# Decoder layer with routed experts: last block routed as two units, maxima loaded by ScalarE, w2 made the stationary operand, last expert by halves

## Chip, cores and metric
One core of a Trainium2 chip runs one program that does the whole layer. The metric is the device time of one execution in microseconds (us). Before the change the median of three runs is 755.97 us (755.29 to 756.68). Lower is better.

## What is computed
The reference is one decoder layer over 8 sequences of 256 tokens (2048 tokens, width 256). Three parts follow each other, each on the layer-normed sum of what came before:

```python
x = x + mixer(layernorm(x))            # projections, depthwise conv, cumprod/cumsum scan, gates
x = x + attention(layernorm(x), ctx, ctx)   # 16 heads of 16, causal, softmax over keys, output projection
xf = layernorm(x)                      # router and experts; the result is combined + xf
probs = softmax(xf @ router_w.T);  k_probs, k_idx = top_k(probs, 2)
rank  = running count of earlier pairs sent to the same expert;  keep = rank < 641
buf[expert, rank] = xf[token]          # 8 experts, 641 slots (648 in the kernel)
out_buf = silu(buf @ w1) @ w2          # w1 256x1024, w2 1024x256 for each expert
combined[token] = sum over its 2 experts of k_prob * out_buf[expert, rank]
```

The change touches the end of the attention stage, the routing and the experts. The mixer is as before.

## The kernel before
The engines have instruction streams of their own, written out by hand, and wait for each other by semaphores (`wait_ge`). Two functions follow each other: `mixer_and_projections` and `attention_route_experts`; all of the change lies in the second and in two small helpers.

**Attention** is a software pipeline over 48 steps `t`, three for each of 16 groups `g` (a sequence and half of its heads; `b` is a sequence, g = 2b or 2b + 1). In a step TensorE (PE) writes the masks, multiplies keys by queries into the bank `a_turned` (`turned`, L1538), computes the scores of the step six ahead (`scores`, L261), and multiplies probabilities by values (`weigh`, L1556). ScalarE (ACT) takes the exponential of `a_turned` (`exps`, L1420). There is one such bank, so the steps run in a ring: exponential, masks, `turned`, exponential. VectorE (DVE) takes the maxima of the scores six steps ahead (L275); every third step it turns them (L288), SyncE (SP) stores them to DRAM (`store_maxima`, L215), issues four large loads of queries and keys (`lay`, L208) and then loads the maxima as two extra query rows (`load_maxima`, L223), for which the first `turned` of that group waits.

At the end of a group DVE transposes the output bank (L1699), GpSimd (POOL) divides by the sums (`divide`, L1339), DVE turns back (L1707), and after two groups PE does the output projection of the sequence (`project`, L1573). The residual, the statistics, the power on POOL (L1328), the normed rows on ACT (L1425), their transposes on PE (`x3_turn`, L1583), the logits (L1593), the choice of two experts on DVE (`choose`, L1732 to L1746), the ranks on PE (`ranks`, L1603 and L1606), the slots (`place`) and the gates are done for blocks of four tiles of 128 tokens, `NBLK` = 4 blocks of two sequences. All of these share one PSUM bank (`a_shared`). A table of step offsets (`PROJECT`, `STATS`, ... `SEND`) says in which step an engine does each. Eight indirect DMAs for each block (`scatter`, L1349) then put the rows into the buffer `disp` in DRAM, and `base` (POOL, L1333) adds the residual that SP stores to `out`.

**Experts.** SP waits for all scatters, then fetches expert 0's rows (`fetch`). PE transposes them (`turn`, L1615), and for each expert goes through 8 pieces `f` of the hidden width: `hidden` (12 matmuls of 324 columns, L101), then `result` (L1649) of the piece before. All products are split in a high and a low part, three matmuls for one. `result` holds the activations as stationary operand, 108 slots at a time, and moves 256 columns of w2: 6 slot tiles x 3 = 18 matmuls a piece. ACT and DVE make silu and its high and low parts (L1457, L1802, L1463, L1808), POOL the odd low half (`low`, L1367) and the low part of the next expert's w1 (L1356). At an expert's end ACT and DVE scale the six tiles by the gate (L1472, L1814), and POOL adds them to `out` by six indirect DMAs (`give`, L1378), the first of which waits until those of the expert before have landed.

## Time and profile before
| | |
|---|---|
| median of three runs | 755.97 us |
| profiled execution, its own time | 752.37 us |
| its span (first to last instruction) | 750.7 us |
| PE, DVE, ACT, POOL busy | 83%, 65%, 46%, 44% |
| mean granted TensorE clock | 0.909 of full speed |
| mean DMA rate | 109 GB/s |
| mixer and projections | to about 270 us |
| attention and routing | about 270 to 470 us |
| experts on PE | about 470 to 734 us |
| last indirect DMAs | 737 to 751 us |

Busy time is the time in which an engine has an instruction in work. PE's matmuls overlap, so that the duration of one (283 ns for L1649) is longer than the distance to the next. A clock of 1.00 is 2.4 GHz, 0.50 is 1.2 GHz; the two are told apart by windows. "Idle before" at an instruction is the time that its engine had nothing to do, with what ended it. Times inside the trace are counted from the start of the span.

### The profile page before, as it was taken

Reading aid. Unit: us, or ns where it says so; the run is one execution under the profiler, and the core shown is the slowest. Engines: PE = TensorE matmul, PEld = TensorE weight load, DVE = VectorE, ACT = ScalarE, POOL = GpSimd, SP = SyncE. Lnnn points to the kernel's source line nnn. Section 1 sums busy time; section 2 is a strip of 40 time slices with the busy share of each in tenths; the row PEclk is TensorE's granted clock in tenths of the full one; section 3 lists DMA queues with packets and bytes.
Section 4 is the critical chain, followed back from the end, with each engine's and each line's share of the span. In section 5 each row is a group of like instructions: output and inputs, shape, how many; then the busy total and the mean of one; then the engine's idle time right before and its main releaser. Section 6 shows DMA issues by size and latency. Waiting matters only on the chain.

```text
span 750.7 us, 12394 instructions
## 1 busy us (share of the span) xinstructions
PE 623.4 (83%) x4408; PEld 524.0 (70%) x4408; DVE 490.3 (65%) x1017; ACT 343.3 (46%) x666; POOL 333.1 (44%) x321
## 2 busy tenths in 40 slices
PE   3586998988986788888889640999999999999991
PEld 2465887877774644555555430899999999999991
DVE  5686687796797545776756430477877777777630
ACT  4565563751633023353524310456555555665540
POOL 1234424233240051122352764245766868677665
PEclk9798999999999579998987855799999999999996
DMA  8301404855338746663661612405263452621123
GB/s 272 99 7 48 115 29 125 270 161 140 86 73 214 168 102 141 153 149 101 170 178 33 208 45 81 146 1 156 29 167 90 102 164 28 167 26 19 19 30 42
DMA packets 63197, 81.68 MB, mean 109 GB/s; under 512 B 10283, under 2 KB 47926, under 8 KB 63136
## 3 DMA queue, kind: packets, MB, share of 16 engines
q1 hardware_dynamic: 53920, 73.08, 34.7%
q0 software_dynamic: 9216, 7.81, 7.3%
q8 instruction: 35, 0.57, 0.3%
q14 instruction: 26, 0.21, 0.1%
HBM read 48.27 MB, written 34.36 MB: 110 GB/s over the span
## 4 chain that ended last, share of the span: by engine, by line
PE 42%; issue 5%; DMA 4%; DVE 4%; SPq 4%; POOL 3%; ACT 1%; POOLq 0%; DVEq 0%; ACTq 0%
PE w_bank L1649 16%; PE l_scores L101 10%; PE w_bank L101 5%; PE a_shared L1573 3%; DMA l_hi<-md 2%; POOL out L1378 2%; PE a_out L1556 2%; SPq L208 2%; PE a_turned L1538 2%; PE l_scores L1615 1%; PE a_shared L1593 1%; PE a_turned L1524 1%; DVE l_nm L275 1%; DMA w_rows<-disp 1%; PE l_scores L261 1%
## 5 line engine op out<-in xcount | busy, mean ns | idle before, releaser
L1649 PE MATMUL w_bank<-w_w2h,l_hi 128*108 128x256 f32 x384 | 108.5, 283 | 0.6 <-POOL l_lo L1367 0.5
L1649 PE MATMUL w_bank<-w_w2h,l_lo 128*108 128x256 f32 x384 | 107.7, 280 | 0.0
L1649 PE MATMUL w_bank<-w_w2l,l_hi 128*108 128x256 f32 x384 | 107.6, 280 | 0.0
L1367 POOL TENSOR_TENSOR l_lo<-w_v,l_hi 128x324 fp32r<-128x324 f32 x64 | 56.3, 879 | 91.7 <-ACT l_hi L1463 91.7
L1420 ACT ACTIVATE a_pr<-a_turned 128x1024 f32<-128x1024 f32 x48 | 49.2, 1024 | 88.4 <-PE a_turned L1538 88.4
L275 DVE TENSOR_REDUCE l_nm<-l_scores 128x4 f32<-128x1024 f32 (+1 forms) x48 | 58.5, 1218 | 37.9 <-PE l_scores L261 37.2
L1378 POOL DMA_INDIRECT out<-w_y,w_to x48 | 75.9, 1582 | 13.3 <-issue 9.9
L1802 DVE SCALAR_TENSOR_TENSOR w_v<-w_th,l_scores 128x324 f32<-128x324 f32 x86 | 42.3, 491 | 49.9 <-ACT w_th L1457 48.6
L1457 ACT ACTIVATE w_th<-l_scores 128x324 f32<-128x324 f32 x86 | 38.1, 442 | 68.6 <-PE l_scores L101 67.7
L1649 PEld LDWEIGHTS w_bank<-w_w2h,l_hi 128*108 128x108 f32 x384 | 66.0, 172 | 1.1 <-issue 1.1
L1463 ACT ACTIVATE l_hi<-w_v 128x324 fp32r<-128x324 f32 x128 | 60.4, 472 | 12.1 <-DVE w_v L1802 11.1
L1649 PEld LDWEIGHTS w_bank<-w_w2l,l_hi 128*108 128x108 f32 x384 | 65.9, 172 | 0.0
L1649 PEld LDWEIGHTS w_bank<-w_w2h,l_lo 128*108 128x108 f32 x384 | 65.9, 172 | 0.0
L1778 DVE TENSOR_TENSOR w_w2l<-w_s,w_w2h 128x256 fp32r<-128x256 f32 x56 | 62.2, 1110 | 1.9
L1356 POOL TENSOR_TENSOR w_w1l<-w_s,w_w1h 128x256 fp32r<-128x256 f32 x64 | 56.8, 888 | 0.0
L101 PE MATMUL l_scores<-l_hi,w_w1h 128*128 128x324 f32 x172 | 54.2, 315 | 1.1 <-ACT l_hi L1452 1.1
L101 PE MATMUL l_scores<-l_lo,w_w1h 128*128 128x324 f32 x172 | 54.4, 316 | 0.0
L101 PE MATMUL l_scores<-l_hi,w_w1l 128*128 128x324 f32 x172 | 54.4, 316 | 0.0
L1339 POOL TENSOR_TENSOR a_on<-a_po,a_rc 128x256 f32<-128x256 f32 x16 | 9.9, 619 | 95.1 <-DVE a_rc L1701 74.8
L101 PE MATMUL l_scores<-m_sh,l_hi 128*128 128x512 f32 x96 | 39.9, 416 | 10.3 <-ACT m_sh L565 6.9
L476 POOL TENSOR_TENSOR m_gl<-m_acc,m_gh 128x512 fp32r<-128x512 f32 x16 | 24.5, 1531 | 37.4 <-ACT m_gh L591 37.4
L467 POOL TENSOR_TENSOR m_rstd<-m_ve,c_mhalf 128x4 f32<-128x4 f32 (+1 forms) x7 | 8.3, 1188 | 70.9 <-DVE m_ve L118 70.9
(233 smaller groups left out, 1710.5 us busy)
## 6 DMA issues: line engine op xcount, KB each, us to landing
w_s<-in_L_ffn_w SPq DMA_DIRECT2D x14, 1024.0 KB, 5.0
l_lo<-kd SPq DMA_DIRECT2D x32, 200.0 KB
l_hi<-qd SPq DMA_DIRECT2D x32, 192.0 KB
disp<-c_blank SPq DMA_DIRECT2D x8, 658.1 KB
w_rows<-disp SPq DMA_DIRECT2D x8, 658.1 KB
kd<-l_qkh SPq DMA_DIRECT2D x16, 256.0 KB, 4.6
vd<-m_vf SPq DMA_DIRECT2D x4, 1024.0 KB, 6.8
qd<-l_qkh SPq DMA_DIRECT2D x16, 256.0 KB, 3.7
```

What stands on the lines that cost most here:

```text
L101: mm = pe.matmul(out, a, b, start=first and n == 0, stop=last and n == 3 * len(parts) - 1)
L275: dve.tensor_reduce(dst, src, AX.X, ALU.max).then_inc(A["nm"], 1)
L476: pool.tensor_tensor(out[:, n, :], src, high[:, n, :].bitcast(F32), ALU.subtract).then_inc(S[name], 1)
L1356: pool.tensor_tensor(w1_piece(w1l, f), w1_piece(s1[e % 2], f), w1_piece(w1h, f).bitcast(F32), ALU.subtract)\
L1367: pool.tensor_tensor(hl[:, g % 3, half(1)], v[:, n % 4, :], hh[:, g % 3, half(1)].bitcast(F32), ALU.subtract)\
L1378: pool.indirect_dma_start(out=out, out_offset=bass.IndirectOffsetOnAxis(ap=to[:, e % 3, t:t + 1], axis=0), in_=y[e % 2][:, t, :], in_offse ...
L1420: act.activation(pr[n % 3][:, :], tbank[:, :], ACT.Exp, scale=SCALE).then_inc(A["exp"], 1)
L1457: act.activation(th[:, n % 2, :], hb[n % 3][:, 0:HALF], ACT.Tanh, scale=0.5).then_inc(F["th"], 1)
L1463: act.activation(hh[:, g % 3, half(u)], v[:, n % 4, :], ACT.Copy).then_inc(F["hh"], 1)
L1649: mm = pe.matmul(eb[t // 2][0:SP_, (t % 2) * D:(t % 2 + 1) * D], a[:, g % 3, s], w2_piece(b, f), start=f == 0 and t % 2 == 0 and n == 0, s ...
L1778: dve.tensor_tensor(w2_piece(w2l, f), w2_piece(s2[e % 2], f), w2_piece(w2h, f).bitcast(F32), ALU.subtract)\
L1802: dve.scalar_tensor_tensor(v[:, n % 4, :], th[:, n % 2, :], 1.0, hb[n % 3][:, 0:HALF], ALU.add, ALU.mult).then_inc(F["v"], 1)
```

## The change
It has six parts.

1. **Maxima loaded by ACT.** `load_maxima` of groups 2 to 15 is issued from ACT's stream behind `exps` of step 3g - 2, no longer from SP behind `lay`. The store's semaphore is split in two by the parity of g.
2. **Other steps.** The offsets become a table by unit. `ranks` of the first blocks goes one step later and ahead of `scores`, `place` to the head of DVE's step, odd `x3_turn` behind `weigh`.
3. **Last block as two units.** Unit 3 is the seventh sequence, unit 4 the eighth: statistics, choice, ranks, slots and four scatters each. Their projection, transposes, logits and ranks use the score banks, which are free by then. `base` of the last block goes behind the last scatter on POOL; SP's order (store of that base, wait for the scatters, fetch) is unchanged.
4. **Expert 0's rows in halves.** Two DMAs; `hidden(0)` stands behind the transposes of the first. `fetch(1)` now waits for expert 0's transposes.
5. **w2 stationary.** `result` holds a 128x128 piece of w2 and moves 324 columns of activations: 2 x 3 x 2 = 12 matmuls a piece into four banks. The result is transposed, so ACT and DVE copy it out (`result_out`), PE transposes it back in 12 transposes an expert (`turn_result`), and then it is scaled as before. `hidden` has two banks in place of three.
6. **Last expert by halves.** For expert 7 all 8 pieces of the first 324 slots come first, then those of the rest. Expert 6's six `give` stand in steps 2, 2, 3, 4, 4, 5 (before: 1 to 6), expert 7's first three in steps 6, 7, 7, the other three behind the loop.

```diff
 # the table: old offsets from 12 * block, new per unit
-    PROJECT, STATS = 9, 10
-    POWER, OFFSET, NORM, TURN, BASE, LOGITS = 17, 18, 19, (20, 22), 22, 23
-    CHOOSE, RANKS, PLACE, WEIGHTS, SEND = 24, 25, 26, 29, 30
+    names = ("project", "stats", "power", "offset", "norm", "turn", "logits", "choose", "ratio", "ranks", "place", "weights", "send")
+    first = ((9, 15), (10, 16), 17, 18, (19, 20), (20, 22), 23, 24, 25, 26, 26, 28, tuple(range(29, 29 + TPB * K)))
+    for row in (((33, 39), (34, 40), 41, 42, (42, 43), (43, 44), 45, 46, 47, 47, 47, 47, (47, 47, 49, 49, 50, 50, 52, 52)),
+                ((44,), (45,), 45, 46, (46,), (47,), 48, 49, 50, 51, 51, 52, (53, 53, 54, 54)),
+                ((50,), (50,), 51, 52, (52,), (53,), 54, 55, 56, 56, 57, 56, (58, 58, 59, 59))):
+    LATE = (2, 2, 3, 4, 4, 5)
...
 # SP
-                    load_maxima(sp, A, lead, md, g)
...
                 store_base(NBLK - 2)
                 store_base(NBLK - 1)
                 sp.wait_ge(R["sent"], 16 * K * NT)
-                fetch(0)
+                fetch_first()
                 fetch(1)
...
 # POOL
+                base(NBLK - 1)
                 low(0)
...
-                        if e > 0 and 1 <= f <= ST:
-                            give(e - 1, f - 1)
-                for t in range(ST):
+                        if e > 0:
+                            for t in range(ST):
+                                if f == (t + 2 if e < E - 1 else LATE[t]):
+                                    give(e - 1, t)
+                        if e == E - 1 and f in (6, 7):
+                            for t in ((0,), (1, 2))[f - 6]:
+                                give(e, t)
+                for t in range(ST // 2, ST):
                     give(E - 1, t)
...
 # ACT
+                    if t % 3 == 1 and 2 <= (t + 2) // 3 < GR:
+                        load_maxima(act, A, lead, md, (t + 2) // 3)
+                def result_out(e, u):
+                    act.wait_ge(F["r"], FC * (e + 1) - (FC // 2 if e == E - 1 and u == 0 else 0))
+                    ge(act, F["yt"], 3 * e)
+                    act.activation(yt[:, 0, half(u)], eb[u][:, 0:HALF], ACT.Copy).then_inc(F["ye_act"], 1)
...
 # PE
+                            mm = pe.transpose(tb[t // 2 % 2][0:SP_, (t % 2) * D + k * P:(t % 2) * D + (k + 1) * P],
+                                              yt[:, k, t * SP_:(t + 1) * SP_], c["ident"][:, :])
...
-                            mm = pe.matmul(eb[t // 2][0:SP_, (t % 2) * D:(t % 2 + 1) * D], a[:, g % 3, s], w2_piece(b, f),
+                            for w, a in ((w2h, hh), (w2h, hl), (w2l, hh)):
+                                for q in part:
+                                    mm = pe.matmul(eb[2 * k + u][:, 0:HALF], w2_piece(w, f)[:, k * P:(k + 1) * P], a[:, g % 3, half(q)],
```

**First place: SP and ACT around one store of maxima.** Before, on SP: `l_mt` is the turned maxima, `md` their place in DRAM, `qd` and `kd` queries and keys.

```order
L215 DMA md<-l_mt 4x32x32 [waits a_mx]
L208 DMA l_hi<-qd 48x4x256 [waits a_st]
L208 DMA l_hi<-qd 48x4x256
L208 DMA l_lo<-kd 50x4x256 x2
L223 DMA l_hi<-md 2x1024 [waits a_md]
L223 DMA l_hi<-md 2x1024
```

Now, on ACT, between two exponentials (L1466 is L1420 of before, L1494 the high part of a w2 piece):

```order
L1466 ACTIVATE a_pr<-a_turned 128x1024 [waits a_pv,a_st] x2
L1494 ACTIVATE w_w2h<-w_s_0 128x256 [waits f_p2_1]
L1466 ACTIVATE a_pr<-a_turned 128x1024 [waits a_pv,a_st]
L223 DMA l_hi<-md 2x1024 [waits a_md1]
L223 DMA l_hi<-md 2x1024
```

The load no longer stands behind four issues on SP; it stands in the stream that the exponentials come from, with its wait for the store.

**Second place: POOL around the last division of the attention (the second `a_on<-a_po,a_rc` below).** Before:

```order
L1339 TENSOR_TENSOR a_on<-a_po,a_rc 128x2x8x16 [waits a_o,a_rc,a_po]
L1356 TENSOR_TENSOR w_w1l<-w_s_0,w_w1h 128x2x128 [waits f_w1h]
L1349 DMA disp<-w_x,w_si 5184x260
L1333 TENSOR_TENSOR g_x<-g_x,w_x 128x1024 [waits w_x3]
L1349 DMA disp<-w_x,w_si 5184x260 x2
L1339 TENSOR_TENSOR a_on<-a_po,a_rc 128x2x8x16 [waits a_o,a_rc,a_po]
L1361 TENSOR_TENSOR w_w2l<-w_s_0,w_w2h 128x256 [waits f_w2h0]
L1349 DMA disp<-w_x,w_si 5184x260 x2
```

Now:

```order
L1376 TENSOR_TENSOR a_on<-a_po,a_rc 128x2x8x16 [waits a_o,a_po]
L1366 TENSOR_TENSOR w_rstd<-w_ve,c_mhalf 128x2 [waits w_ve]
L1393 TENSOR_TENSOR w_w1l<-w_s_0,w_w1h 128x2x128 [waits f_wh]
L1386 DMA disp<-w_x,w_si 5184x260
L1371 TENSOR_TENSOR g_x<-g_x,w_x 128x1024 [waits w_x3]
L1386 DMA disp<-w_x,w_si 5184x260 x2
L1386 DMA disp<-w_x,w_si 5184x260 [waits r_wr,r_si,w_xb]
L1386 DMA disp<-w_x,w_si 5184x260
L1376 TENSOR_TENSOR a_on<-a_po,a_rc 128x2x8x16 [waits a_o,a_po]
L1398 TENSOR_TENSOR w_w2l<-w_s_0,w_w2h 128x256 [waits f_wh]
L1386 DMA disp<-w_x,w_si 5184x260 x5
L1366 TENSOR_TENSOR w_rstd<-w_ve,c_mhalf 128x2 [waits w_ve]
```

Between the last two divisions there now stand the power of unit 3, with its wait for the variance, and the first two scatters of the third block, with their wait for slots and gates.

**Third place: PE in `result`, the start of expert 0's first piece.** Before (banks 4 to 6, output 108x256):

```order
L1649 MATMUL w_bank4<-w_w2h,l_hi 108x256 [waits f_hl_odd,f_hl,f_w2l0]
L1649 MATMUL w_bank4<-w_w2l,l_hi 108x256
L1649 MATMUL w_bank4<-w_w2h,l_lo 108x256
L1649 MATMUL w_bank4<-w_w2h,l_hi 108x256
L1649 MATMUL w_bank4<-w_w2l,l_hi 108x256
```

Now (banks 4 to 7, output 128x324):

```order
L1758 MATMUL w_bank4<-l_hi,w_w2h 128x324 [waits f_hl_odd,f_hl,f_wl]
L1758 MATMUL w_bank5<-l_hi,w_w2h 128x324
L1758 MATMUL w_bank4<-l_lo,w_w2h 128x324
L1758 MATMUL w_bank5<-l_lo,w_w2h 128x324
L1758 MATMUL w_bank4<-l_hi,w_w2l 128x324
```

A piece takes 12 of these where it took 18, each with more columns.

## Rows read from the trace of the kernel before
**Rows 1.** Windows: length; PE, PEld, DVE, ACT, POOL busy (count); clock, DMA share, GB/s.
```profile
556.25:588.60 32.35, 32.35 (x255) 32.33 (x254) 24.84 (x50) 18.98 (x49) 23.56 (x23) 1.00 0.44 108
```
**Rows 2.** The chain of waits in the experts: start us, length us, what.
```profile
643.23 1.79 PE l_scores L101 x12
645.02 2.11 PE w_bank L1649 x18
```
**Rows 3.** Timeline of PE around transposes: start, length, engine, line, operation, tiles.
```profile
412.44 0.66 PE L1583 MATMUL a_shared<-c_ident,w_x 128*128 128x128 f32 x4
413.03 0.64 PE L1556 MATMUL a_out<-a_pr,l_lo 128*32 128x256 f32 x8
560.00 0.72 PE L1615 MATMUL l_scores<-c_ident,w_rows 108*128 108x108 f32 x6
560.68 0.28 PE L1649 MATMUL w_bank<-w_w2l,l_hi 128*108 128x256 f32 x1
```
**Rows 4.** Timeline of one piece: last hidden matmul, then POOL.
```profile
697.84 0.32 PE L101 MATMUL l_scores<-l_hi,w_w1l 128*128 128x324 f32 x1
699.76 0.88 POOL L1367 TENSOR_TENSOR l_lo<-w_v,l_hi 128x324 fp32r<-128x324 f32 x1 [0.43 <-ACT l_hi L1463]
701.71 1.58 POOL L1378 DMA_INDIRECT out<-w_y,w_to  x1 [0.19 <-issue]
```
**Rows 5.** Timeline of the attention: a store and load of maxima, and PE's waits.
```profile
305.78 0.57 SPq L215 DMA_DIRECT2D md<-l_mt  x1
309.41 0.73 SPq L223 DMA_DIRECT2D l_hi<-md  x2
313.98 0.50 PE L1538 MATMUL a_turned<-l_hi,l_lo 50*128 50x256 f32 x4 [1.42 <-DMA l_hi<-md]
389.78 0.35 PE L1603 MATMUL a_shared<-w_both,c_onesb 128*128 128x32 bf16 x7 [2.73 <-issue]
```
**Rows 6.** Who waited for whom: us in total, times, longest.
```profile
PE a_turned L1538 <- DMA l_hi<-md: 6.6, 5, 1.9
```
**Rows 7.** The chain of waits: projections of the attention, then the routing of the last block.
```profile
355.85 1.92 PE a_shared L1573 x8
373.91 1.92 PE a_shared L1573 x8
398.03 3.71 PE a_shared L1573 x8
430.22 3.52 PE a_shared L1573 x8
433.83 0.70 DVE g_x L1713
436.29 1.05 POOL w_rstd L1328
442.33 3.59 PE a_shared L1593 x16
460.85 2.10 DMA disp<-w_x,w_si
462.96 5.38 DMA w_rows<-disp
```
**Rows 8.** Timeline of POOL at the end of the attention and in the routing.
```profile
425.24 0.97 POOL L1349 DMA_INDIRECT disp<-w_x,w_si  x1 [0.30 <-issue]
427.11 0.61 POOL L1339 TENSOR_TENSOR a_on<-a_po,a_rc 128x256 f32<-128x256 f32 x1 [0.90 <-DVE a_po L1699]
442.67 2.36 POOL L1333 TENSOR_TENSOR g_x<-g_x,w_x 128x1024 f32<-128x1024 f32 x1
451.91 0.97 POOL L1349 DMA_INDIRECT disp<-w_x,w_si  x1 [1.89 <-DVE w_x L1757]
```
**Rows 9.** Timeline of POOL at the program's end.
```profile
732.12 1.58 POOL L1378 DMA_INDIRECT out<-w_y,w_to  x1 [0.21 <-issue]
737.07 1.58 POOL L1378 DMA_INDIRECT out<-w_y,w_to  x1 [3.38 <-DMA out<-w_y,w_to]
746.48 1.57 POOL L1378 DMA_INDIRECT out<-w_y,w_to  x1 [0.30 <-issue]
```

More of the change, by code:

```diff
@@ L1389, in _ @@
                         divide(t // 3 - 1)
-                    if due(t, POWER) is not None:
-                        power(due(t, POWER))
-                    if due(t, BASE) is not None:
-                        base(due(t, BASE))
+                    for i in units(t, "power"):
+                        power(i)
+                    if t in BASE:
+                        base(BASE.index(t))
                     if t % 6 == 3 and 1 <= t // 6 <= FC:
@@ L1397, in _ @@
                         low_first_w2(t // 6 - 1)
-                    for n in range(TPB * K):
-                        if due(t, SEND + n) is not None:
-                            scatter(due(t, SEND + n), n)
+                    for i in range(NU):
+                        for n, x in enumerate(steps[i]["send"]):
+                            if x == t:
+                                scatter(i, n)
+                base(NBLK - 1)
                 low(0)
@@ L1503, in _ @@
                             high(2 * g + 3)
+                        if e > 0 and f in (1, 2):
+                            result(e - 1, 4 * (f - 1))
+                            result(e - 1, 4 * (f - 1) + 1)
                         if e + 1 < E:
@@ L1508, in _ @@
                                 turned(e + 1, 2 * (f - 3) + 1)
-                    for t in (0, 1, 4, 5):
-                        result(e, t)
+                        if e == E - 1 and f == 4:
+                            result_out(e, 0)
+                        if e == E - 1 and f == 5:
+                            result(e, 0)
+                            result(e, 1)
+                    if e < E - 1:
+                        result_out(e, 0)
+                    result_out(e, 1)
+                for t in (4, 5):
+                    result(E - 1, t)
             @block.tensor
@@ L1664, in _ @@
                         turned(t)
+                    for i in units(t, "ranks"):
+                        if i < NBLK - 2:
+                            ranks(i)
                     if u < NS:
                         scores(pe, A, lead, u)
[L1667 to L1675 removed]
+                    for b in pairs(t, "project"):
+                        project(b)
+                    for b in pairs(t, "turn"):
+                        if b % 2 == 0 and b < B - 2:
+                            x3_turn(b)
+                    for i in units(t, "logits"):
+                        if i < NBLK - 1:
+                            logits(i)
                     if 1 <= t <= NS:
                         weigh(t - 1)
[L1678 to L1679 removed]
+                    for b in pairs(t, "turn"):
+                        if b % 2 == 1 or b == B - 2:
+                            x3_turn(b)
+                    for i in units(t, "logits"):
+                        if i >= NBLK - 1:
+                            logits(i)
+                    for i in units(t, "ranks"):
+                        if i >= NBLK - 2:
+                            ranks(i)
+                turn(0, 0)
+                turn(0, 1)
                 hidden(0)
+                turn(0, 2)
+                turn(0, 3)
+                hidden(1)
                 for e in range(E):
@@ L1818, in _ @@
                     u = t + LEAD
+                    for i in units(t, "place"):
+                        place(i)
                     if u < NS:
@@ L1851, in _ @@
                             low(g + 1)
+                        if e > 0 and f == 1:
+                            result(e - 1, 2)
+                            result(e - 1, 3)
                         if f > 0 and e + 1 < E:
```

427 lines of the change are left out of this document (248 added, 179 removed).

## Prediction
> **What bounds the kernel now.** I read the windows by stage first, then the chain of waits, then the timeline at the places where the chain changes engine. In the 32.35 us of one expert PE is busy for 32.35 at full clock, DVE for 24.84, ACT for 18.98, POOL for 23.56 [rows 1]: only PE's work sets the time there. In the attention nobody is full. The chain goes round the ring of exponential, masks and `turned`, and is broken by two kinds of wait: `turned` for the loaded maxima (five times, 6.6 us together [rows 6], one of them 1.42 us [rows 5]), and `ranks`, for which PE stands 2.73 us until DVE has chosen [rows 5]. After the second kind the clock is low: the projection then takes 3.71 us where it takes 1.92 [rows 7]. The routing of the last block is one serial chain of small steps over all engines, from 430.2 to the rows' arrival at 468.3 [rows 7]. At the end POOL's six indirect adds of expert 7 wait for those of expert 6 [rows 9].
>
> All sums are made against the profiled execution, 752.37 us (span 750.7). The median of the runs, 755.97, lies 3.6 higher; I add that at the end.
>
> **Term 1, w2 stationary.** 18 matmuls of 256 columns take 2.11 us, 117 ns each; 12 of 324 columns take 1.79, 149 ns each [rows 2]. `result` becomes 12 of the latter. A piece goes from 3.90 to 3.58 us, 0.32 less. Up to the step in which the tail (term 4) begins, 62 pieces: 19.8 us. Against it stand 12 new transposes an expert, 7 experts up to there, 84. Two durations bound them, as distances and not as lengths. Four transposes of 128 columns pass from 412.44 to 413.03, 148 ns each. Six of 108 columns pass from 560.00 to about 560.56 (the second matmul behind, at 560.68, less one distance of 117), 94 ns [rows 3]. The new ones have 128 columns of identity and 108 of data. I take the middle, 125 ns: 10.5 us (bounds 7.9 and 12.4). Net 9.3 less.
>
> Can the others follow at 3.58 us a piece? The slack of the longest chain: the last hidden matmul starts at 697.84, POOL's low half ends at 700.64, 2.8 us; the `result` that needs it starts 1.79 + 1.79 = 3.58 later, so 0.8 us are left (before 1.1) [rows 4]. POOL has 0.88 for it and 1.58 for a `give` in the same step; over an expert its 23.56 us fit into the new 31.2. DVE's 24.84 [rows 1] grows by two copies of some 0.4 to 25.6. `hidden` loses a bank: it now needs the gate of two halves earlier, which has a whole `result` of time. I give back 0.6 in all. **Term 1: -8.7** (-11.9 to -3).
>
> A length is easily read for a distance here: the single matmul behind the transposes stands with 0.28 us [rows 3], though the next starts 0.12 later. The Trainium skill, "TensorE: Matmul & The Clock Gate", section on PE-mode transpose, gives about 275 ns for one in a kernel's context. By that figure the 84 would cost 23.1 us and term 1 would be +3.3 + 0.6, by the distances in [rows 3] it is -8.7; the trace does not agree with it as a distance.
>
> **Term 2, the attention.** (a) The load of maxima is issued 3.63 us after its store, behind four issues of `lay` [rows 5], and the data are used 4.5 us after that. From ACT it can go as soon as the store has landed. Of 6.6 us of waiting I take 5 back. The Trainium skill, "DMA: Bandwidth & Descriptors", section "Issuing engines are not separate DMA queues", says that another issuing engine saves only the sequencer's time, since all DMAs run on the same 16 engines. By that the gain is the time of `lay`'s issues, most of the 3.63 less the store's landing, which would leave something of each wait; by the row's distance, if the load also overtakes `lay`'s data, it is all of 6.6. (b) `ranks` one step later: from projection to projection it is 18.1 us without `ranks` and 24.1 with [rows 7], and the latter holds 1.9 us of logits; leaves 4.2 for this block. The block with `ranks` before it went alike, somewhat less. But these blocks had no wait for maxima, because the low clock gave the load its time; without a stall such waits come up. I take 8 for both blocks together with small waits of `x3_turn`, which now stands behind `weigh`. (c) Lost: nothing on ACT if its two issues (0.73 on SP [rows 5]) lie in its idle time between two exponentials. `place` now stands ahead of the maxima on DVE, once a block; I hold that within (b). **Term 2: -13** (bounds -18.6, all of 6.6 and twice the 6.0 between the blocks, and -3).
>
> **Term 3, routing.** Logits half as many at the low clock: 3.59 to 1.8; choice, gates and normed rows for two tiles save some 0.5 + 0.8 + 0.7. From the residual (433.83) to the first scatter (451.91) it was 18.1, it becomes 13.7 with 0.5 for POOL's late power. The scatters stand 1.28 apart; 7 distances become 3: from 8.9 to 3.8. But `base` (2.36 [rows 8]) now stands between the last scatter and SP's store, and SP fetches behind that: from the last scatter's start to the fetch it was 2.1 (460.85 to 462.96 [rows 7]), it becomes 0.97 + 2.36 + 0.5 = 3.9. Sum from the residual: 29.1 becomes 21.4, 7.7 less.
>
> What stands ahead grows. Before, POOL was free at 426.2 and waited 0.90 us for the last division at 427.11 [rows 8]. Now power 3 waits for its variance (1.0 by my count of the steps) and takes 1.05 [rows 7], and two scatters take 2.56: 4.6 more, less 0.9 of slack. The projection starts as late behind the division as before, 3.1 us, less 1.8 since `choose` of the third block has moved ahead of it; but it also starts later against the steps, and at the low clock (3.52). I count 2.8 us later for the residual. Entry to the experts: `store_base` now goes just ahead of the half rows, the first half lands after 5.4 us or a little more, and `hidden(1)` comes behind the transposes of the second: 1.0 later. **Term 3: -7.7 + 2.8 + 1.0 = -4** (-11 to +2: without any delay at the division, or with a clock and store that cost twice).
>
> **Term 4, the end.** Expert 7's first `give` waits for the landing of expert 6's last: 732.12 to 737.07, 4.95 us; then six, 1.88 apart, and 4.2 after the last start at 746.48 [rows 9]. It stays six behind that wait: expert 6's last now stands in step 5 of 8, one piece earlier, and by my count PE is done with the second half before POOL comes to it. So the halves of expert 7 gain nothing by themselves; the earlier last `give` gains one piece, 3.6 to 4, less 1.3 for two doubled steps. **Term 4: -3** (-1 to -5).
>
> Sum: -8.7 - 13 - 4 - 3 = -28.7: 723.7 against 752.4, and with the 3.6 of the median 727.3, rounded to 727.
>
> **Rivals.** A, *the attention keeps its pace.* The load gains its issue time, but DVE's `place` in front of the maxima and the new ring of waits eat it, and the logits and ranks stay as long. For it: ring steps without any wait set most of the 18.1 us. Then term 2 is -4, and the time 736. B, *nothing is late in the routing*: power 3 does not wait, the division starts at once and the projection finds the full clock. Term 3 is -11, the time 720. Against it: POOL's order. C, *slower*: ACT stands in front of the next exponential until the store has landed, in each of 14 groups. The whole path from store to load's issue is 3.63 us [rows 5]; if all of it stood in the ring, 14 x 3.63 = 50.8, against 23.7 of the other terms (without the 5 of the maxima): 783. It decides from 1.7 us a group (23.7 / 14). Against it: three ring steps lie between the store and the data's use, 8.2 us in [rows 5], and the load is placed behind the first, by when a store of this size should have landed. D, *the new transposes do not overlap*: each costs a full length, for which the nearest row has 0.28 us [rows 3]. Term 1 is 84 x 0.28 - 19.8 + 0.6 = +4.3, the time 740. The distances in [rows 3] speak against it, a clock that falls behind a group of transposes would speak for it. The Trainium skill's figure for a transpose, named under term 1, is of this size. E, *the change does not do what it says*: DVE or POOL becomes the bound of the experts at 3.8 us a piece, and 62 x 0.22 = 13.6 are lost: 741. With DVE at 25.6 of 31.2 us possible, not likely.
>
> **Numbers.** Forecast 0.60, A 0.16, B 0.10, C 0.04, D 0.03, E 0.07. Predicted is the likeliest, 727 us. The range for eight of ten is 712 to 740: below, B with term 2 near its lower bound; above, A with a third of term 1 lost, or D. The forecast's own range is 720 to 734. A measurement of this kernel tells about 0.2% (1.5 us) from no change. All cases but C lie far below that: faster 0.95, within 0.2% 0.01, slower 0.04.
>
> **What would show it.** Right: pieces of 3.58 us and `result` of 1.79 with PE at 100%; transposes 95 to 150 ns apart; PE's wait for maxima under 2 us in all; no wait of PE in `ranks` of the first three blocks, and a clock near 1.00 over the whole attention; the last division some 5 us behind the last `weigh`; the fetch 3.9 us behind the last scatter's start; six `give` in a row behind one landing. Wrong: exponentials that start late behind ACT's DMA issues (C), a granted clock below 1.00 in the experts (D), waits of `result` for POOL or DVE (E), or 18 us from projection to projection without any wait for DMA (A).

## The result, and the profile after

| | before | changed |
|---|---|---|
| median of 4 runs, us | 756.33 (755.29 to 757.85) | 737.63 (735.39 to 738.82) |
| profiled execution, us | 752.37 | 736.82 |
| its span, us | 750.7 | 735.0 |

The changed kernel takes 0.9748 of the time before (95% interval 0.9717 to 0.9779): 18.7 us less by the medians, 15.7 less by the two profiled spans. The forecast was 727, the range 712 to 740, and rival A, the attention that keeps its pace, stood at 736. The two traces, cut where both have the same instruction:

| stretch | before | changed | gain | predicted |
|---|---|---|---|---|
| start to the end of the last `weigh` | 424.70 | 422.96 | -1.7 | -13 |
| to the last residual (DVE adds it) | 433.83 | 432.30 | +0.2 | +2.8 |
| to the fetch of the rows | 462.96 | 454.44 | -7.0 | -7.7 |
| to the first `result` | 478.91 | 470.60 | +0.2 | +1.0 |
| 56 pieces, to expert 7's first `result` | 705.82 | 692.51 | -5.0 | -8.3 |
| to the last add's start | 746.48 | 730.34 | -2.8 | -3.4 |
| to the end | 750.7 | 735.0 | +0.4 | 0 |

The end of `weigh` is that of its last record (423.62 + 1.08 and 421.88 + 1.08; in the kernel before its release reaches DVE only at 425.94). The profiled execution of the kernel before lies 4.0 us under its median, that of the changed one 0.8: the medians have 3.0 us more between them than this table, and no trace shows in which stretch.

(Of term 1's sum, 56 pieces carry 56 x 0.32 = 17.9 less 72 transposes of 125 ns = 9.0, less the 0.6 given back; its other 6 pieces, 0.4 net, stand in the tail's -3.4.)

The experts first. Windows of three experts, from the first `result` of one to that of the next (columns as in [rows 1]):

```profile
532.46:564.15 31.69, 31.48 (x216) 30.84 (x217) 25.67 (x52) 19.92 (x51) 23.47 (x23) 1.00 0.43 109
564.15:595.87 31.72, 31.51 (x216) 30.86 (x217) 25.63 (x52) 19.90 (x51) 23.46 (x23) 1.00 0.45 110
595.87:628.29 32.42, 31.47 (x216) 30.82 (x217) 26.40 (x52) 20.17 (x51) 24.22 (x23) 1.00 0.44 109
```

Against [rows 1] the length is 31.7 in two of them, and in the third no less than before, with PE idle for 0.95. What PE waits for stands in its timeline, here with DVE's and POOL's rows of the same moment:

```profile
564.15 0.38 PE L1758 MATMUL w_bank<-l_hi,w_w2h 128*128 128x324 f32 x1 [0.21 <-DVE w_yt L1947]
...
567.83 1.03 PE L1715 MATMUL l_scores<-c_ident,w_yt 128*108 128x128 f32 x8
568.62 0.54 PE L1758 MATMUL w_bank<-l_hi,w_w2h 128*128 128x324 f32 x2
...
625.41 0.95 POOL L1404 TENSOR_TENSOR l_lo<-w_v,l_hi 128x324 fp32r<-128x324 f32 x1
625.56 1.78 DVE L1909 TENSOR_TENSOR w_w2l<-w_s,w_w2h 128x256 fp32r<-128x256 f32 x1
626.26 0.79 POOL L1393 TENSOR_TENSOR w_w1l<-w_s,w_w1h 128x256 fp32r<-128x256 f32 x1
627.26 0.88 DVE L1947 COPY w_yt<-w_bank 128x324 f32<-128x324 f32 x2
628.29 0.39 PE L1758 MATMUL w_bank<-l_hi,w_w2h 128*128 128x324 f32 x1 [0.95 <-DVE w_yt L1947]
```

Eight of the new transposes pass in 568.62 - 567.83 = 0.79 us, 99 ns each, near the lower of the two distances of [rows 3]. Their length in the trace is 272 ns. A `result` takes 1.77 to 1.80 us. So both durations of term 1 are right, and the loss lies elsewhere: the first `result` of an expert waits until DVE has copied the finished banks (`result_out`), and DVE has those two copies behind the split of a w2 piece, whose subtraction takes 1.78 us in two of the experts, beside two POOL operations that follow each other, and 0.97 to 1.1 elsewhere.

In the attention PE's waits have changed their name (who waited for whom, PE, from 286 to 430 us; to be held against [rows 6]):

```profile
PE l_scores L261 <- DMA l_lo<-kd: 4.7, 5, 1.4
PE a_turned L1585 <- ACT a_pr L1466: 4.4, 15, 0.5
PE a_turned L1599 <- DMA l_hi<-md: 2.0, 2, 1.4
```

The maxima cost 2.0 us instead of 6.6, and `scores` now waits 4.7 us for k, which it never did before. `turned` of group g and `scores` of group g + 2 stand next to each other in one step; the first waits for the maxima, the second for the loads of q and k issued right behind the store of these maxima. The early wait had hidden the later one. Together the two are 6.7 us, as much as the maxima alone before.

The clock is the other half of the prediction for the attention. The same window of both traces, before and now:

```profile
286.00:425.00 139.00, 118.26 (x1176) 71.59 (x1173) 85.53 (x215) 57.11 (x77) 41.44 (x47) 0.91 0.54 141
286.00:425.00 139.00, 123.27 (x1198) 75.27 (x1196) 93.37 (x250) 58.77 (x81) 44.31 (x51) 0.89 0.55 146
```

PE no longer waits in `ranks` of the first two blocks, where it had waited 2.2 and 2.7 us, and yet the granted clock is 0.89 where it was 0.91, and not near 1.00 as forecast.

DVE and POOL at the end of the attention (timeline; first the last `weigh` of the kernel before, then the changed kernel; the row that stands in [rows 8] at 427.11 is at 427.23 here):

```profile
423.62 1.08 PE L1556 MATMUL a_out<-a_pr,l_lo 128*32 128x256 f32 x24
```
```profile
418.06 2.71 DVE L1868 TENSOR_TENSOR w_d<-w_m 128x4 f32<-128x4 f32 x1
418.38 2.36 POOL L1371 TENSOR_TENSOR g_x<-g_x,w_x 128x1024 f32<-128x1024 f32 x1
...
421.45 0.46 PE L1674 MATMUL a_shared<-w_both,c_onesb 128*128 128x32 bf16 x11 [1.85 <-DVE w_both L1876]
...
421.88 1.08 PE L1617 MATMUL a_out<-a_pr,l_lo 128*32 128x128 f32 x16
...
424.02 0.71 DVE L1830 STREAM_TRANSPOSE a_po<-a_out 128x512 f32<-128x512 f32 x1
...
424.97 0.97 POOL L1386 DMA_INDIRECT disp<-w_x,w_si  x1 [1.79 <-DVE w_x L1888]
426.25 0.97 POOL L1386 DMA_INDIRECT disp<-w_x,w_si  x1 [0.30 <-issue]
427.23 0.64 POOL L1376 TENSOR_TENSOR a_on<-a_po,a_rc 128x256 f32<-128x256 f32 x1
```

The third block's routing now lies in the last steps of the attention. DVE's subtraction w_d, of four numbers a partition, takes 2.71 us beside POOL's `base`; `ranks` waits 1.85 for it, the last `weigh` stands behind `ranks`, DVE's transpose stands behind `place` and the gates, and the division behind two scatters: 4.3 us from the end of `weigh` to the division, where it was 2.4. The projection then starts 1.2 us behind the division (428.41), where it was 3.1.

The fetch and what stands ahead of it (chain of waits; before: [rows 7, 8]):

```profile
450.64 0.97 POOL disp L1386
451.63 2.37 POOL g_x L1371
454.01 0.38 SPq L1320
454.40 0.04 issue
454.44 4.50 DMA w_rows<-disp
```

From the last scatter's start to the fetch it is 3.80 us (predicted 3.9), `base` and its store in between. And the end (timeline of POOL; before: [rows 9]):

```profile
715.90 1.58 POOL L1417 DMA_INDIRECT out<-w_y,w_to  x1 [0.19 <-issue]
720.90 1.58 POOL L1417 DMA_INDIRECT out<-w_y,w_to  x1 [2.29 <-DMA out<-w_y,w_to]
730.34 1.58 POOL L1417 DMA_INDIRECT out<-w_y,w_to  x1 [0.30 <-issue]
```

Again six adds in a row behind one landing.

### The profile page after: what moved, and what is told of

Same layout as the page of the kernel before. It is cut to its first block, busy times and chain, and to the rows that moved or that the text cites. A ratio compares the mean times of both kernels' runs of the same rounds, so it can differ in the third digit from the quotient of the medians.

```text
span 735.0 us, 11954 instructions
## 1 busy us (share of the span) xinstructions
PE 619.0 (84%) x4134; PEld 514.1 (70%) x4134; DVE 502.8 (68%) x1055; ACT 350.2 (48%) x683; POOL 333.6 (45%) x322
## 4 chain that ended last, share of the span: by engine, by line
PE 38%; DVE 6%; DMA 5%; issue 5%; POOL 4%; SPq 3%; ACT 1%; another core or an unknown queue 0%; DVEq 0%; POOLq 0%; ACTq 0%
PE w_bank L1758 13%; PE l_scores L101 13%; DMA l_lo<-kd 3%; PE a_shared L1637 2%; POOL out L1417 2%; PE l_scores L1692 2%; PE a_out L1617 2%; SPq L208 1%; DMA l_hi<-md 1%; PE l_scores L1715 1%; PE a_turned L1599 1%; PE a_turned L1585 1%; PE l_scores L261 1%; PE l_scores L1637 1%; PE a_shared L1662 1%
## 5 line engine op out<-in xcount | busy, mean ns | idle before, releaser
L1935 DVE SCALAR_TENSOR_TENSOR w_v<-w_th,l_scores 128x324 f32<-128x324 f32 x128 | 62.0, 490 | 56.0 <-ACT w_th L1505 54.1
L1466 ACT ACTIVATE a_pr<-a_turned 128x1024 f32<-128x1024 f32 x48 | 49.1, 1022 | 80.8 <-PE a_turned L1599 80.8
L101 PE MATMUL l_scores<-l_hi,w_w1h 128*128 128x324 f32 x256 | 81.2, 317 | 2.3 <-DVE l_lo L1927 1.2
L101 PE MATMUL l_scores<-l_hi,w_w1l 128*128 128x324 f32 x256 | 81.0, 316 | 0.0
L275 DVE TENSOR_REDUCE l_nm<-l_scores 128x4 f32<-128x1024 f32 (+1 forms) x48 | 58.3, 1216 | 28.6 <-PE l_scores L261 27.5
L1758 PE MATMUL w_bank<-l_hi,w_w2h 128*128 128x324 f32 x256 | 64.3, 322 | 3.7 <-DVE w_yt L1947 2.8
L1758 PE MATMUL w_bank<-l_lo,w_w2h 128*128 128x324 f32 x256 | 61.3, 310 | 0.0
L1758 PE MATMUL w_bank<-l_hi,w_w2l 128*128 128x324 f32 x256 | 61.2, 310 | 0.0
L101 PEld LDWEIGHTS l_scores<-l_hi,w_w1h 128*128 128x128 f32 x256 | 49.2, 192 | 2.9 <-ACT l_hi L1500 2.9
L101 PEld LDWEIGHTS l_scores<-l_hi,w_w1l 128*128 128x128 f32 x256 | 49.4, 193 | 0.0
L101 PEld LDWEIGHTS l_scores<-l_lo,w_w1h 128*128 128x128 f32 x256 | 49.3, 193 | 0.0
L101 PE MATMUL l_scores<-m_sh,l_hi 128*128 128x512 f32 x96 | 40.0, 416 | 10.3 <-ACT m_sh L565 6.9
L1758 PEld LDWEIGHTS w_bank<-l_hi,w_w2h 128*128 128x128 f32 x256 | 42.6, 189 | 5.6 <-issue 3.2
L1758 PEld LDWEIGHTS w_bank<-l_hi,w_w2l 128*128 128x128 f32 x256 | 43.7, 188 | 0.0
```

The costliest lines, as they stand in the source:

```text
L101: mm = pe.matmul(out, a, b, start=first and n == 0, stop=last and n == 3 * len(parts) - 1)
L275: dve.tensor_reduce(dst, src, AX.X, ALU.max).then_inc(A["nm"], 1)
L1466: act.activation(pr[n % 3][:, :], tbank[:, :], ACT.Exp, scale=SCALE).then_inc(A["exp"], 1)
L1758: mm = pe.matmul(eb[2 * k + u][:, 0:HALF], w2_piece(w, f)[:, k * P:(k + 1) * P], a[:, g % 3, half(q)], start=f == 0 and n == 0, stop=f == ...
L1935: dve.scalar_tensor_tensor(v[:, n % 4, :], th[:, n % 2, :], 1.0, hb[n % 2][:, 0:HALF], ALU.add, ALU.mult).then_inc(F["v"], 1)
```

## The experiments

Ratios are to the kernel before on the same chip; the changed kernel has 0.9748 (0.9717 to 0.9779). One per cent is 7.6 us. For parts of a kernel I compare stretches of the traces. The attention itself is not steady: its seventh projection starts at 406.42 us in the changed kernel and between 402.5 and 411.9 in the seven other profiles whose attention is the same up to there, so a single profile says nothing of a few microseconds of attention; there I go by the timed medians.

**The changed kernel again** (`changed_again`).

> The changed kernel once more, word for word, beside the other runs of this set. All theories: 2.5% below the kernel before on the same chip, as in its first measurement, and the profile with PE's waits for maxima and for k of 6 to 7 us together in the attention. It shows how far the granted clock and the ring of the attention differ between two executions of one program: I expect the last residual within 4 us of 432.3.

738.68 us, 0.9758 (0.9691 to 0.9824). PE waited 4.0 us for k and 1.2 for maxima. The last residual came at 434.10, 1.8 later, as expected. The two waits are 5.2 us together, somewhat under the expected 6 to 7.

**The loads of the maxima back on SP** (`load_on_sp`).

```
                         lay(sp, A, M, lead, qd, kd, g + 2)
...
+                    load_maxima(sp, A, lead, md, g)
...
-                    if t % 3 == 1 and 2 <= (t + 2) // 3 < GR:
-                        load_maxima(act, A, lead, md, (t + 2) // 3)
```

> The changed kernel with the loads of the maxima back on SP, behind the four loads of q and k, as before. My step in the prediction (the waits of 6.6 us for maxima lose 5): this kernel is then 4 to 5 us slower than the changed one, about 742. Theory after the result (waits exchanged, 6.6 us for maxima against 2.0 + 4.7): PE waits 5 to 7 us for maxima and hardly for k, and the time is within 2 us of the changed kernel, 736 to 740.

741.66 us, 0.9835 (0.9763 to 0.9908): some 6 us slower than the changed kernel by the ratios (4.0 by the medians, on different chips); the intervals just overlap, so the size is uncertain by as much as itself. PE no longer waits for k, and for the maxima more than either theory said:

```profile
PE a_turned L1598 <- DMA l_hi<-md: 9.7, 5, 3.3
```

9.7 us against 2.0 + 4.7, and against 6.6 in the kernel before. So within the new order ACT's load is worth about what I had expected. Against the kernel before it is not: there 6.6 us of waits became 6.7.

**q and k ahead of the maxima** (`lay_first`).

```
-                    store_maxima(sp, A, lead, md, g)
                     if g + 2 < GR:
                         lay(sp, A, M, lead, qd, kd, g + 2)
+                    store_maxima(sp, A, lead, md, g)
```

> The changed kernel, with the loads of q and k for group g + 2 issued on SP ahead of the store of the maxima of group g, instead of behind it. Theory (the wait was exchanged): in the changed kernel PE waits 2.0 us for maxima and 4.7 us in `scores` for k; both are due in the same step, so taking time from the one showed the other. The loads of q and k have their buffer some 3 us before the store can go, so they now land some 3 us earlier: the waits for k (4.7 us) go to near 0, those for the maxima stay under 3 us, and the attention is 4 to 6 us shorter: about 732 against 737.6. Rival (the ring sets the pace): without the wait for k the same time is spent between exponential, mask and `turned`, and the time stays within 1.5 us of the changed kernel. Rival on the other side: the four issues (2.9 us) hold the store back, the maxima come later, PE waits over 6 us for them, and the time is 2 to 5 us longer than the changed kernel's.

745.58 us, 0.989 (0.9809 to 0.9971): some 10 us slower than the changed kernel. The wait for k is gone and that for the maxima is 0.7 us, as the theory said, and still it loses. The reason is in ACT's waits and its timeline:

```profile
ACT a_pr L1466 <- DMA md<-l_mt: 6.7, 2, 4.4
ACT w_x L1472 <- DMA md<-l_mt: 5.0, 2, 2.7
ACT w_ex L1485 <- DMA md<-l_mt: 3.1, 1, 3.1
```
```profile
290.09 0.56 SPq L215 DMA_DIRECT2D md<-l_mt  x1
...
294.67 0.54 ACTq L223 DMA_DIRECT2D l_hi<-md  x2
...
296.73 1.02 ACT L1466 ACTIVATE a_pr<-a_turned 128x1024 f32<-128x1024 f32 x1 [2.85 <-PE a_turned L1599]
```

With 0.8 MB of q and k issued ahead of it the store of 16 KB has landed 4.6 us after its issue (4.0 to 5.1 for the groups 2 to 13; in the changed kernel 2.0 to 2.5 for most, 4.0 in two), and ACT stands in front of its load for 14.8 us in all. PE's waits for ACT (the exponential and the normed rows) grow with it, from 4.4 + 1.5 us in the changed kernel to 8.2 + 5.2. This is rival C of the prediction: it sleeps in the changed kernel, and a small change of the order on another engine wakes it.

**`ranks` one step earlier** (`ranks_early`).

```
-    first = ((9, 15), (10, 16), 17, 18, (19, 20), (20, 22), 23, 24, 25, 26, 26, 28, tuple(range(29, 29 + TPB * K)))
+    first = ((9, 15), (10, 16), 17, 18, (19, 20), (20, 22), 23, 24, 25, 25, 26, 28, tuple(range(29, 29 + TPB * K)))
```

> The changed kernel with PE's `ranks` of the first two blocks back in step 25 of 12, one step ahead of where it stands (DVE's `place` stays in step 26). My step in the prediction (4.2 us a block are lost in the stall and the low clock behind it): PE again waits 2.5 us or more for DVE twice, some projections fall to 3.6 us, and the time is 5 to 9 us longer, 743 to 746. Rival (the ring sets the pace, the stall lies beside it or stands in for a wait for DMA): at most 3 us longer.

This is not the place that `ranks` had before: there it stood in step 25 too, but behind `scores`, the projection and the logits; here it stands ahead of `scores`.

750.13 us, 0.9955 (0.9922 to 0.9989): 15 us slower, twice what I had expected, and far from the rival's 3. The two stalls are there, and they alone are 4.0 us:

```profile
346.89 0.24 PE L1674 MATMUL a_shared<-w_both,c_onesb 128*128 128x24 bf16 x3 [2.44 <-DVE w_both L1876]
393.35 0.35 PE L1674 MATMUL a_shared<-w_both,c_onesb 128*128 128x32 bf16 x7 [1.55 <-DVE w_both L1876]
```

Of the rest a part goes with the clock. The windows from 286 to 425 us of the changed kernel, of `ranks_early` and of the next kernel:

```profile
286.00:425.00 139.00, 123.27 (x1198) 75.27 (x1196) 93.37 (x250) 58.77 (x81) 44.31 (x51) 0.89 0.55 146
```
```profile
286.00:425.00 139.00, 123.38 (x1142) 74.85 (x1144) 85.96 (x212) 55.63 (x75) 36.85 (x43) 0.86 0.53 140
```
```profile
286.00:425.00 139.00, 122.19 (x1072) 74.31 (x1073) 82.77 (x205) 52.68 (x71) 36.83 (x43) 0.80 0.49 126
```

PE is busy equally long in all three, but with 1198, 1142 and 1072 matmuls at a granted clock of 0.89, 0.86 and 0.80. After the first stall a projection takes 3.78 us. By the clock alone `ranks_early` would lose 139 x (1 - 0.86 / 0.89) = 4.7 us in this window (an estimate), so that 8.7 of the 10.3 us by which its seventh projection is later (416.76, 406.42) are accounted for. That the stalls lower the clock is not shown: the kernel before has 4.9 us of them and 0.91.

**Both undone** (`both_undone`: the two edits above in one kernel).

> The changed kernel with both attention edits undone: the loads of the maxima on SP behind those of q and k, and `ranks` of the first two blocks in step 25. Undone alone, the first cost 0.8% (some 6 us) and the second 2.0% (some 15 us). If they are independent, this kernel takes 757 to 760 us, no less than the kernel before, and the seventh projection starts at 419 to 424. If they share one stall (the wait for maxima lies in the time that the stalled `ranks` and the low clock give the load, as in the kernel before), it takes 745 to 752 us, with the seventh projection at 411 to 417: one step less than the 415.2 of the kernel before.

753.42 us, 1.0003 (0.9967 to 1.0039). That is some 19 us over the changed kernel, where the two undone alone make 6.6 + 15.7 = 22 by the ratios, each uncertain by several us: the sum within the noise, and the seventh projection, at 422.6, lies where the sum had it (419 to 424). One shared stall (745 to 752 us, 411 to 417) is out.

The time equals that of the kernel before, but by a different way. The last `weigh` ends at 441.28, 16.6 us later than in the kernel before; from there to the end it is 310.1 us, 15.9 less. So the new order, without its two attention edits, costs the attention some 16 us against the kernel before: PE waits 8.7 us for maxima (before 6.6), and the clock is 0.80 (before 0.91). By the seventh projection (422.6, before 415.2 with a step of some 2.9 us more in front of it) it is 10 us, half of it in the two stretches with `ranks`. The place of `ranks` ahead of `scores`, which this kernel keeps, is a cause that was not tested; so are the odd `x3_turn` behind `weigh` and the new position of the third block. This also means that 6 and 15 us price the two edits inside the new order; they are not what the edits gained over the kernel before.

**`place` back behind the maxima** (`place_behind`).

```
                     for i in units(t, "place"):
-                        place(i)
+                        if i >= NBLK - 1:
+                            place(i)
...
                         turn_back(t // 3 - 1)
+                    for i in units(t, "place"):
+                        if i < NBLK - 1:
+                            place(i)
```

> The changed kernel with DVE's `place` of the first three blocks back behind the maxima, the division and `turn_back` of its step (as in the kernel before), `ranks` still in step 26. It asks why the changed kernel with the loads and `ranks` undone takes 753.4 us, the same as before, though its routing, experts and tail are some 14 us shorter in the trace: its attention is 8 to 10 us longer. Theory P (`place` ahead of the maxima holds DVE, and through it the scores, once a block, for 1 us and the low clock behind it): the time falls by 2 to 6 us, to 732 to 736 at 756 before, ratio 0.969 to 0.973. Theory Q (what costs is the rest of the new order on PE, the turns and logits behind `weigh`, or the clock): within 1.5 us of the changed kernel, ratio 0.974 to 0.977. Rival R (the early `place` is worth something, since PE's next projection waits for it): 2 to 5 us longer.

736.23 us, 0.9787 (0.9723 to 0.9851). No gain; the interval holds the changed kernel's ratio and reaches only the upper edge of theory P's 0.969 to 0.973. Theory P finds no support, and what costs the rest stays open.

**`base` and its stores last** (`bases_last`).

```
-    BASE = (22, 34, 46)
+    BASE = (22, 34)
...
+                base(NBLK - 2)
                 base(NBLK - 1)
...
-                store_base(NBLK - 2)
-                store_base(NBLK - 1)
                 sp.wait_ge(R["sent"], 16 * K * NT)
                 fetch_first()
+                store_base(NBLK - 2)
+                store_base(NBLK - 1)
```

> The changed kernel with POOL's additions `base` of the third and the last block both behind the last scatter, and SP's two stores of them behind the fetch of the first expert's rows. Theory: (a) the fetch no longer stands behind `base` (2.37 us) and its store: 2.8 us earlier; (b) DVE's subtraction w_d, which took 2.71 us beside POOL's `base` of the third block and 0.55 in the blocks before, falls under 1 us, and with it the choice, the scatters and the last division come 1 to 2 us earlier. Together 4 to 5 us less: about 733. Rival 1 (w_d is long for another reason, (b) is nothing): 2.4 to 2.8 us less, 735. Rival 2 (the stores of 512 KB each and `base` now stand beside the rows' landing and the first low halves, and hold them up): no gain or a loss, 737 to 740.

731.57 us, 0.9704 (0.9636 to 0.9773): 3.3 us below by the ratio, with intervals that overlap; the theory's 733 is 0.970, rival 1's 735 lies inside the interval too. The trace is plainer. From the last scatter's start to the fetch it is 447.95 - 445.83 = 2.12 us instead of 3.80; the landing takes no longer. So (a) brings 1.7 of its 2.8 us. And w_d, without POOL's `base` beside it:

```profile
415.71 0.15 DVE L1869 TENSOR_TENSOR w_d<-w_m 128x4 f32<-128x4 f32 x1
```

0.15 us instead of 2.71. That is contention of the two engines, and not the operation. Less of it reaches the division than (b) had: from the seventh projection to the last division it is 20.1 us, where the changed kernel has 20.8 and, run again, 23.0. The Trainium skill, "SBUF — State Buffer", section "SBUF: two separate sides", has a mechanism: VectorE and GpSimd share one pair of ports as an exclusive lock, also for a VectorE operation with two inputs in SBUF against a GpSimd operation that reads SBUF; the one that starts first has it for its whole instruction, and the other stands. The traces agree at the end of the wait: w_d ends 0.03 us after `base` (420.77, 420.74). They do not at its start: w_d's record begins 0.32 us before `base`'s, and alone it would have been done by then.

**The third block's `ranks` behind the last `weigh`** (`route2_late`).

```
-    for row in (((33, 39), (34, 40), 41, 42, (42, 43), (43, 44), 45, 46, 47, 47, 47, 47, (47, 47, 49, 49, 50, 50, 52, 52)),
+    for row in (((33, 39), (34, 40), 41, 42, (42, 43), (43, 44), 45, 46, 47, 48, 49, 48, (49, 49, 50, 50, 52, 52, 53, 53)),
```

> The changed kernel with the third block's `ranks` in step 48 (behind the last `weigh` on PE), its gates in 48, `place` in 49 and its first two scatters in 49 instead of 47. Theory: in the changed kernel the last `weigh` stands behind `ranks` of the third block, which waits 1.8 us for DVE, and the last division stands behind two scatters that wait for `place` and the gates (4.5 us from the last `weigh` to the division). Both go: the last division starts 4 to 5 us earlier. POOL then has the two scatters more behind it and becomes the bound of the routing, so that 1.5 to 3 us of this are left at the fetch: 734 to 736 where the changed kernel has 737.6. Rival (POOL's 16 scatters set the end of the routing): nothing is left, within 1 us.

736.95 us, 0.9736 (0.9661 to 0.9811), beside `changed_again` at 738.68: not to be told apart, as the rival has it. From the seventh projection to the last division it is 19.0 us instead of 20.8 (23.0 in `changed_again`), and from there to the last scatter 25.6 instead of 23.4. What the division gains, POOL's scatters take back.

**DVE's copies first** (`copy_first`).

```
+                        if f == FC - 1 and e < E - 1:
+                            result_out(e, 0)
+                            result_out(e, 1)
                         if f > 0 and e + 1 < E:
                             split_w2(e + 1, f - 1)
```

> The changed kernel with DVE's two copies of the finished result (`result_out`) ahead of the split of the last w2 piece of the step, instead of behind it. Theory: PE's wait at the start of each next expert (0.21 us five times less, 0.95 twice, 2.8 us in all) comes from DVE's order; in the experts where POOL's work stands beside it the subtraction w_w2l takes 1.78 us for 0.7. Then every expert takes 31.0 to 31.5 us instead of 31.7 or 32.4, and the time falls by 2 to 3 us. Rival (PE cannot start the first `result` earlier, since the low half of hidden is as late): under 1 us.

733.84 us, 0.9701 (0.9634 to 0.9768); 4.8 us below `changed_again` on the same chip, and the runs of the two do not overlap (732.53 to 735.44, 737.37 to 739.96). An expert takes 31.2 to 31.3 us, each of them:

```profile
531.28:562.48 31.20, 31.20 (x218) 30.80 (x217) 25.31 (x51) 19.85 (x51) 23.30 (x23) 1.00 0.44 111
```

PE is full again. (The subtraction takes 0.97 to 1.1 us in the changed kernel where it is not 1.78, and not 0.7 as I had expected; here the seven that meet no POOL operation take 0.43 to 0.47.) From the first `result` to PE's last it is 245.3 us instead of 249.9 (716.98 - 471.71, 720.48 - 470.60): more than the predicted 2 to 3.

**Expert 6's adds a step earlier** (`late`).

```
-    LATE = (2, 2, 3, 4, 4, 5)
+    LATE = (1, 2, 2, 3, 3, 4)
```

> The changed kernel with POOL's six indirect adds of expert 6 in steps 1, 2, 2, 3, 3, 4 of expert 7 instead of 2, 2, 3, 4, 4, 5. Theory (the end is set by POOL's queue and the landing of expert 6's last add): this landing comes about 3.6 us, a step, earlier, the wait of 2.29 us at 720.9 goes, one to three adds of expert 7 run before PE ends, and the last add starts 2 to 4 us earlier. Rival (POOL's low halves stand behind the doubled adds, and PE's last pieces wait for them, 0.8 us once in the changed kernel): PE ends 2 us or more later, and the time is the same or longer.

740.29 us, 0.9759 (0.9674 to 0.9844): no difference that can be told. From the first `result` to the last add's start it is 258.1 us instead of 259.7, so 1.6 gained, short of the expected 2 to 4. The wait for the landing is gone, but POOL's order has a low half in front of expert 7's first add:

```profile
725.88 0.87 POOL L1404 TENSOR_TENSOR l_lo<-w_v,l_hi 128x324 fp32r<-128x324 f32 x1 [2.84 <-ACT l_hi L1511]
726.94 1.58 POOL L1417 DMA_INDIRECT out<-w_y,w_to  x1 [0.19 <-issue]
```

**Three edits together** (`three`), **and with the earlier adds** (`three_and_late`).

> The changed kernel with three of the edits tried alone, together: `base` of the third and last block behind all scatters and their stores behind the fetch; `ranks`, gates and `place` of the third block one or two steps later; DVE's result copies ahead of the split of w2. Alone they had ratios of 0.970, 0.974 and 0.970 to the kernel before, where the changed one had 0.975. If the gains add: 4 + 1 + 4 us, 728 to 730 us at 756 before, ratio 0.963 to 0.966. Expected rows: experts of 31.25 us, the fetch by 447. Rival (the first two meet in POOL's scatters): 0.967 to 0.970.

> The same three edits and the adds of expert 6 a step earlier (1, 2, 2, 3, 3, 4), which alone made no difference that could be told, though its last add came 1.6 us earlier against the first `result`. Expected: 1 to 2 us below the kernel with the three edits, if POOL's lows keep up at 31.25 us an expert; the same time otherwise.

727.24 us, 0.9662 (0.9589 to 0.9734), and 728.74 us, 0.9648 (0.957 to 0.9727). Both are faster than the kernel before, and by the medians than the changed one (735.39 its lowest run, 729.43 the highest of the eight), though the intervals of the ratios just overlap with its own. The ratio of `three` lies at the edge of what adding gains would give (0.963 to 0.966), below the rival's 0.967. In `three` the rows are fetched 43.7 us after the seventh projection (448.99 - 405.29; changed: 48.0), at 449 and not by 447, and the experts take 31.2 to 31.3 us. The early adds add nothing that can be told.

## Why the prediction was right, and where not

The time lies in the range, beyond the likeliest case's own 720 to 734, and near rival A's 736. The gain from trace to trace is 15.7 us where the stretches had 28.6: 11.3 of the missing 12.9 are the attention and 3.3 term 1, against 2.6 that the last residual came sooner. It is nearly the case that I had set above, A with a third of term 1 lost.

- **Term 1, w2 stationary: -8.3 predicted for 56 pieces, -5.0 measured.** `result` of 1.79 and distances of 95 to 150 ns came as forecast; the transposes were even cheaper (99 for 125 ns). What failed is the term's "I give back 0.6": I counted DVE's load over an expert (25.6 of 31.2 us, measured 25.7) and not its order at the one place where PE now needs it at once, the bank that is reused. `copy_first` gives 31.2 instead of 31.7 or 32.4 an expert: 226.9 less 7 x 31.25 is 8.2 us, the predicted size. An engine that has room on average was late in one step out of eight. Rivals D and the strong form of E are out, the weak form of E is what happened.
- **Term 2, attention: -13 predicted, -1.7 measured** (at most 3.0 us more by the medians). Stretches between projections say where.
  - (b), `ranks`: from the third to the fourth projection and from the fifth to the sixth it was 22.8 and 24.1 us and is 20.0 and 20.6, 6.4 less where I had 8; in the changed kernel run again it is 5.7 less, in `late` 1.7. PE has no wait there in the first two blocks; in the third it waits 1.85 us, which I had excluded. And the clock did not rise to 1.00 when the stalls were gone; it is 0.89, before 0.91.
  - The step that failed first is (a): "Of 6.6 us of waiting I take 5 back". The other three stretches up to the sixth projection are no shorter (53.5 us before, 54.1 now), and PE's waits for DMAs went from 6.6 to 2.0 + 4.7.
  - The second that failed is (c), "lost: nothing": from the seventh projection to the end of the last `weigh` it is 16.5 us (18.5 to 18.8 in the three other profiles of this attention) where it was 9.5, and the earlier step of the projection explains only some 2.9 of it. There the third block's choice, `ranks` and logits moved into the last steps.
  - Rival A's sign asked for 18 us between projections without any wait for DMA: the 17.2 to 18.5 us are there, with waits for k in them.
  - What the new order costs beyond this, by `both_undone`, is open; `place` ahead of the maxima shows no part in it.
- **Term 3, routing: -4 predicted, -6.6 measured** (+0.2 - 7.0 + 0.2). The division came 4.3 us behind the last `weigh`, 1.9 later than before, where 3.7 had been worked out; the projection's earlier start behind it took 1.9 back (1.8 predicted). The fetch came 3.8 us behind the last scatter's start (3.9). One sum was off: the savings listed make 14.3 us of the 18.1 from the residual to the first scatter, and 14.8 with POOL's 0.5, not 13.7; it took 14.5 (446.81 - 432.30). I had missed that `base` on POOL stops DVE. Parts 3, 4 and 6 of the change were never undone alone, so what each is worth is read from these stretches and not tested.
- **Term 4, the end: -3.4 predicted with its share of term 1, -2.8 measured**, and 0.4 lost at the very end.
- **Rival C** did not occur: ACT never stood for a store in the changed kernel. `lay_first` shows that the mechanism is real: 14.8 us of ACT's waits beside some 10 us of time.
- The Trainium skill's rule on issuing engines ("DMA: Bandwidth & Descriptors", "Issuing engines are not separate DMA queues"), by which something of each wait would be left, fits: 2.0 us of the wait for maxima were left, and k waited in its place. `load_on_sp`, with 9.7 us of waits, shows that the order of issue still matters.

## What to carry to other kernels

When two loads are due in one step, taking the wait off the first shows the second: look up what the next instruction on the waiting engine needs before counting the gain. When a buffer is handed over, look at the order on the engine that empties it at that place, and not at its load over a period. A transfer's completion that an engine waits for in its own stream should have nothing large issued ahead of it. And an edit undone inside a new order prices it in that order: 19 us for two edits here, in an attention that as a whole gained less than 5.

## What the runs showed of the hardware

- A VectorE subtraction of 128 x 4 elements took 2.71 us beside a 2.36 us GpSimd addition and 0.15 without it; it ended 0.03 us after the addition, though its record began 0.32 us before. One of 128 x 256 took 1.78 beside two GpSimd operations in a row, 0.97 to 1.1 in the other pieces of the changed kernel, and 0.43 to 0.47 in `copy_first` where no GpSimd operation ran.
- Transposes of 108 columns by 128 pass 99 ns apart, though each has a length of 272 ns in the trace.
- A store of 16 KB had landed some 2 us after its issue in most groups, and 4.6 us when four loads of about 200 KB were issued just ahead of it.
- In the attention TensorE's granted clock was 0.91 with 4.9 us of stalls in `ranks`, 0.89 without them, and 0.86 and 0.80 in the two kernels that have `ranks` ahead of `scores` in step 25: its stalls alone do not tell its clock.
